# Clearing attention's query and key slabs on ScalarE during the first expert stage, with batch 0 normalised first and a store wait moved

## The chip, the cores and the metric

The kernel runs on 1 core of a Trainium2 chip. The metric is the device time of one execution in microseconds (us), taken as the median of several runs. The engines are PE (TensorE), DVE (VectorE), ACT (ScalarE), POOL (GpSimd) and SP (SyncE, which here only issues DMAs and waits).

## The reference, cut to what matters

Four residual blocks follow one another on x of shape (8, 512, 128), each behind a layer norm. Only the two in the middle, and the seam between them, are near the change.

```python
x = x + L0_attn(layernorm(x))     # a linear recurrence and a small MLP
x = x + L0_ffn(layernorm(x))      # 8 experts, top 2, gelu, hidden 256
x = x + L1_attn(layernorm(x))     # causal attention, 16 heads of 8
x = x + L1_ffn(layernorm(x))      # 8 experts, top 2, gelu, hidden 512, and a shared one

def L1_attn(x):                   # x: (8, 512, 128)
    q, k, v = heads(x @ Wq.T), heads(x @ Wk.T), heads(x @ Wv.T)
    logits = where(causal, q @ k.T * 8 ** -0.5, -max)
    return merge(softmax(logits) @ v) @ Wo.T
```

## The kernel before, in words

The kernel is a row of blocks (`nc.Block()`): `setup`, `lru_block`, `experts` for layer 0, `attention`, `route`, `experts` for layer 1. In a block each engine has a program of its own; the engines are tied by semaphores alone, and each works through its queue in order. At the end of a block every engine drains, they meet in a barrier, and only then does any of them start the next block.

**The expert stage (layer 0).** Before it tokens are sorted by expert into slots in DRAM (`xslots`), in two groups of four batches. `experts` walks over 10 bodies of 8 tiles. SP loads tiles to `xt`, PE transposes them, multiplies with the first weights into `hb` (gelu on ACT) and with the second into PSUM; DVE copies the result to `yb[r]`, and SP stores `yb[r]` to `yslots` (`store`, L996). At the head of the block DVE still sorts the second group (L319 to L381), POOL scatters its rows, and ACT has two short tasks: an exponential that waits for `exp_in` (L1067) and the first two weight copies (L1051). The first Gelu (L1082) waits for PE. POOL gathers the four batches of group 0 (L902) while the second group is computed, and DVE adds three of them to X at the end. The last thing in SP's program is a wait for both `stored` semaphores (L1028 and L1029): the last rows must have landed in `yslots`, since the next block gathers from there.

**Attention.** The queries and keys go through DRAM: `keep` stores the projected terms, `spread` reads them back, 32 small DMAs a batch, into slabs `Q` [128, 4, 512] and `KZ` [128, 16, 512], of which it fills only some rows. The other rows must be zero (in `KZ` also a constant from `sgn`), and they are written once, at the head of the block, by DVE (L1465, L1467, and four times L1472, one for each 32 partitions). Then DVE copies `identr` and clears `Mc`, and only then come `scales` (the reciprocal of the deviations, which waits for a square root on ACT, L273) and `normalise` for batch 0 (L747 to L752). PE transposes the normalised batch (`turn_in`, L1676), ACT copies it out (`to_xs`, L1600), PE projects keys and queries (L1681), ACT and DVE split each into a high and a low part (`upper`, L1607, and `lower`, L1484), SP stores and spreads them, and PE's first scores (L1695) wait for the first spread. POOL meanwhile clears `Vz` (L1440, L1444), normalises batch 1, lays the values out, and gathers batches 4 to 7 of the expert stage (L902), which DVE adds to X one after another within batch 0.

**Memory.** In the kernel before `Q` and `KZ` are buffers of `attention` alone, `yb` belongs to each expert stage, and `stage` (raw weights, 16 KB a partition) lives from `setup` to the end of the first expert stage.

Of the kernel before, what the change touches and what calls it, by code (L numbers as in the profile page):

```python
# [19 lines left out]
P = 128  # L20
# [3 lines left out]
E = 8  # L24
# [372 lines left out]
def lru_block(nc, s, A, sem, sb):  # L397
# [23 lines left out]
    flat = lambda t: t[:, :, :].rearrange("p j d -> p (j d)")  # L421
    tiles = lambda b: slice(TB * b, TB * b + TB)
    TURNS = B + 2

    RANK = GROUPS[0] + 2

# [508 lines left out]
        batch_stats(dve, s, b, 2)  # L935


def experts(nc, s, sem, layer, out=None):


# [2 lines left out]
    def sems(name, count):  # L943
        return [sem(f"{name}{k}{tag}") for k in range(count)]
# [5 lines left out]
    two = range(2)  # L950
    RING = 4
    scattered, stored = s.scattered, sems("stored", 2)
    sums = s.sums = Sums(sem, layer)

    x_load, loaded = s.x_load, 16 * BODIES * layer
# [29 lines left out]
    with nc.Block() as block:  # L985
        @block.sync
        def _(sp):
            def load(g, n, r):

                wait_apart(sp, x_turned, 2 * (n + BODY0[g]) + (r + 1))  # L990
                sp.dma_start(xt[r][:, :, :], xrows[g][:, bass.ds(BT * n + TB * r, TB), :]).then_inc(x_load[r], 16)

            def store(g, n, r):

                wait_apart(sp, yb_ready, 2 * (n + BODY0[g]) + (r + 3))
                sp.dma_start(yrows[g][:, bass.ds(BT * n + TB * r, TB), :], yb[r][:, :, :]).then_inc(stored[r], 16)  # L996

            def rows_in(g):
                sp.wait_ge(scattered[g], 16 * 2 * TB * GROUPS[g] * (layer + 1))

            rows_in(0)
            for r in two:
                load(0, 0, r)
            for g in range(NG):

                for r in two:
                    load(g, 1, r)
                    if g > 0:
                        store(g - 1, GB[g - 1] - 1, r)
                with sp.Fori(1, GB[g] - 1) as n:  # L1010
                    for r in two:
                        load(g, n + 1, r)
                        store(g, n - 1, r)
                if g + 1 < NG:
                    rows_in(g + 1)
                for r in two:
                    if g + 1 < NG:
                        load(g + 1, 0, r)
                    store(g, GB[g] - 2, r)
            for r in two:  # L1020
                store(NG - 1, GB[NG - 1] - 1, r)
            if layer == 1:

                for b in range(B):
                    sp.wait_ge(x_done, b + 1)
                    sp.dma_start(out[b].rearrange("(j p) d -> p j d", p=P), s.X[:, TB * b:TB * b + TB, :]).then_inc(x_out, 16)
                sp.wait_ge(x_out, 16 * B)
            for r in two:  # L1028
                sp.wait_ge(stored[r], 16 * BODIES)  # L1029

        @block.gpsimd
        def _(pool):
# [12 lines left out]
        def _(act):  # L1045
# [17 lines left out]
                    shared(b)  # L1063

            if layer == 0:
                act.wait_ge(exp_in, 1)
                act.activation(s.top[:, 1, :], s.top[:, 1, :], ACT.Exp).then_inc(exp_ready, 1)  # L1067
                warm(act, s, 0, ACT.Gelu)
                for t, e in enumerate(numbers(act, 0, 2)):
                    copy_down(0, t, e)  # L1070
# [244 lines left out]
def attention(nc, s, sem, sb):  # L1315
# [1 line left out]
    NCH = 5 * HG // 2  # L1317
    names = ("nb_ready", "turned", "xs_ready", "p_ps", "high_ready", "p_ready", "v_ps", "v_ready", "vz_ready", "s_ready",
             "s_read", "m_ready", "mh_ready", "mc_ready", "mt_ps", "q2_ready", "w_ready", "e_ready", "cut", "pv_ready", "o_ready", "ot_ps",
             "rd_ready", "a_ready", "at_ps", "af_ready", "wo_ps", "x_done", "slabs", "vz_zero", "ln_in")  # L1320
    q = {n: sem(n + "_t") for n in names}
    qk_in = [sem(f"qk_in{g}") for g in range(G)]
    kept = [sem(f"kept{k}") for k in range(2)]
    terms = [nc.dram_tensor(f"terms{k}", (B, 3 * P, T), F32, kind="Internal").ap() for k in range(2)]
    Q, KZ = sb("Q", [P, G, T], F32R), sb("KZ", [P, H, T], F32R)
    high, low = [[sb(f"{n}{k}", [P, T], F32R) for k in range(2)] for n in ("high", "low")]
    Vs = sb("Vs", [P, TB, P])
    Vz = sb("Vz", [P, TB, H, SLAB])
# [20 lines left out]
    with nc.Block() as block:  # L1349
        @block.sync  # L1350
        def _(sp):
            def keep(b):

                for k, parts in ((KEY, (high, high, low)), (QUERY, (high, low, high))):
                    wait_apart(sp, q["p_ready"], 2 * b + (k + 1))
                    for t, part in enumerate(parts):
                        sp.dma_start(terms[k][bass.ds(b, 1), P * t:P * t + P, :].rearrange("b p t -> (b p) t"),
                                     part[k][:, :].bitcast(F32)).then_inc(kept[k], 16)

            def spread(b, gg, used):  # L1360

                if gg == 0:
                    for k in (KEY, QUERY):
                        wait_apart(sp, kept[k], WRITES * b + WRITES)
                if used is not None:
                    wait_apart(sp, q["w_ready"], used)
                for g in range(HG):
                    rows = slice(SLAB * g, SLAB * g + 3 * DH)
                    for k, dst in ((QUERY, Q[rows, gg, :]), (KEY, KZ[rows, HG * gg + g, :])):
                        heads = terms[k][bass.ds(b, 1), :, :].rearrange("b (r h) t -> h (b r) t", h=H)  # L1370
                        sp.dma_start(dst.bitcast(F32), heads[G * g + gg, :, :]).then_inc(qk_in[gg], 16)

            sp.wait_ge(q["slabs"], 7)
            keep(0)
            for gg in range(G):
                spread(0, gg, None)
            with sp.Fori(0, B - 1) as b:
                keep(b + 1)
                for gg in range(G):
                    spread(b + 1, gg, NCH * G * b + NCH * (gg + 1))  # L1380
            for gg in range(G):
                sp.wait_ge(qk_in[gg], READS * B)

        @block.gpsimd
        def _(pool):
# [61 lines left out]
            norm_in(1, 1)  # L1447
            norm_rows(0, TB)
            spread(0, None)
            for b in range(FIRST[1], B):  # L1450
                gather(pool, s, s.sums, b)
                if b == B // 2 + 1:
                    norm_in(2, 2)
                    norm_rows(0, TB)
# [7 lines left out]
        @block.vector  # L1462
        def _(dve):
            dve.sem_inc(q["s_read"], 2)
            dve.tensor_copy(Q[:, :, :].rearrange("p G (t c) -> p (G t) c", c=P),  # L1465
                            s.zero[:, :].unsqueeze(1).broadcast_to([P, G * TB, P])).then_inc(q["slabs"], 1)
            dve.tensor_copy(KZ[:, :, :].rearrange("p h (t c) -> p (h t) c", c=P),  # L1467
                            s.zero[:, :].unsqueeze(1).broadcast_to([P, H * TB, P])).then_inc(q["slabs"], 1)
            dve.wait_ge(q["slabs"], 2)
            for g in range(HG):  # L1470
                rows = slab(g)
                dve.tensor_scalar(KZ[rows, g:H:HG, :].rearrange("p h (t c) -> p h t c", c=P),  # L1472
                                  s.zero[rows, :].unsqueeze(1).unsqueeze(1).broadcast_to([SLAB, G, TB, P]), s.sgn[rows, 2:3], None, ALU.add)\
                   .then_inc(q["slabs"], 1)
            dve.tensor_copy(identr[:, :], s.ident[:, :])
            dve.tensor_copy(Mc[:, :, :], s.zero[:, :].unsqueeze(1).broadcast_to([P, TB, P])).then_inc(q["slabs"], 1)
            scales(dve, s, 2)
            normalise(dve, s, nb, s.mu[1], s.r[1], 0, q["ln_in"], 1).then_inc(q["nb_ready"], 1)
            dve.wait_ge(q["slabs"], 7)

            def lower(b, k, ps):

# [380 lines left out]
def build(nc, A, out):  # L1863
    with ExitStack() as ctx:
# [33 lines left out]
        s.x_load = [sem(f"x_load{r}") for r in range(2)]  # L1898

        s.stats_sems = [sem(f"stats_{n}") for n in ("st", "mv", "std", "done")]  # L1900
        s.warmed = sem("warmed")
        s.route_sems = [sem(f"route_{n}") for n in ("exp_in", "exp_ready", "mb_ready", "rank_ps")]
        s.mb_ready, s.rank_ps = s.route_sems[2:4]
        s.rank_read, s.placed, s.route_chain = (sem(n) for n in ("rank_read", "placed", "route_chain"))
# [7 lines left out]
        s.mu, s.r = [sb(f"muc{k}", [P, TB]) for k in range(2)], [sb(f"rc{k}", [P, TB]) for k in range(2)]  # L1912
        s.rd = sb("rd", [P, TB * HG, 2])
        s.nb, s.xs = [sb(f"nb{k}", [P, TB, P]) for k in range(2)], [sb(f"xs{k}", [P, T]) for k in range(2)]
        s.b2row = s.bcast[:, 0:P].unsqueeze(1).broadcast_to([P, TB, P])

        def ffn(layer, start):

            with ExitStack() as own:
# [17 lines left out]
                s.xT = [fs(f"xT{layer}{k}", [P, T]) for k in range(2)]  # L1937
                s.wst = [fs(f"wst{layer}{k}", [P, NC * P]) for k in range(2 * TB)]
                s.hb = [fs(f"hb{layer}{k}", [P, NC * P]) for k in range(4)]
                s.yb = [fs(f"yb{layer}{k}", [P, TB, P]) for k in range(2)]  # L1940
                s.rk = fs(f"rk{layer}", [P, 2 * E * TB * max(GROUPS)])
                start()
                experts(nc, s, sem, layer, out)


# [3 lines left out]
        with ExitStack() as early:  # L1949
            es = allocator(early)  # L1950
            s.w1T, s.w2T = es("w1T", [P, E, F0 * P]), es("w2T", [P, E * F0, P])
            s.stage = es("stage", [P, 2 * E * F0, P])

            def first_stages():
                own_buffers(lambda nc, s, sem, sb: setup(nc, s, A, sem, sb))
                own_buffers(lambda nc, s, sem, sb: lru_block(nc, s, A, sem, sb))

            ffn(0, first_stages)
        own_buffers(attention)
        ffn(1, lambda: route(nc, s, sem))  # L1960


# [19 lines left out]
```

## Time and profile before

| | |
|---|---|
| median of 3 runs | 988.51 us (987.65 to 989.19) |
| the profiled execution | 990.38 us, of which the span from its first to its last instruction is 988.6 us |
| granted TensorE clock, mean over the span | 0.915 of full |
| the experts' last DVE instruction ends, attention's first instructions start | 252.2 us, 256.8 us |
| PE has nothing to do at this seam | 251.5 to 271.9 us |

Times of single instructions are read from the profiled execution, on a clock that starts with its span. An idle time in brackets is that of the engine before the instruction, with what ended it. A granted clock of 0.50 is TensorE at 1.2 GHz, 1.00 is 2.4 GHz.

### The profile page before, as it was taken

Reading aid. Unit: us, or ns where it says so; the run is one execution under the profiler, and the core shown is the slowest. Engines: PE = TensorE matmul, PEld = TensorE weight load, DVE = VectorE, ACT = ScalarE, POOL = GpSimd, SP = SyncE. Lnnn points to the kernel's source line nnn. Section 1 sums busy time; section 2 is a strip of 40 time slices with the busy share of each in tenths; the row PEclk is TensorE's granted clock in tenths of the full one; section 3 lists DMA queues with packets and bytes.
Section 4 is the critical chain, followed back from the end, with each engine's and each line's share of the span. In section 5 each row is a group of like instructions: output and inputs, shape, how many; then the busy total and the mean of one; then the engine's idle time right before and its main releaser. Section 6 shows DMA issues by size and latency. Waiting matters only on the chain. (4 is left out here: it accounts for less than half of the span.)

```text
span 988.6 us, 18788 instructions
## 1 busy us (share of the span) xinstructions
PE 808.0 (82%) x5585; PEld 601.9 (61%) x5585; DVE 637.7 (65%) x1445; ACT 503.9 (51%) x1081; POOL 417.4 (42%) x520
## 2 busy tenths in 40 slices
PE   2798816898159899999999999977278899999993
PEld 2566606898125456565555656546236899999862
DVE  4578643558729987777777777727721566568457
ACT  3475423565114566767767676664122366665520
POOL 3664567547277113232332332221167720273174
PEclk9999857999669999999999999995579899999997
DMA  5920014544144121313122131000012222242222
GB/s 156 366 81 1 30 47 137 160 141 138 30 149 134 44 84 43 99 32 99 44 96 76 51 99 46 17 1 0 6 48 72 94 80 75 81 116 76 78 61 69
DMA packets 82155, 80.45 MB, mean 81 GB/s; under 512 B 9856, under 2 KB 61758, under 8 KB 82110
## 3 DMA queue, kind: packets, MB, share of 16 engines
q1 hardware_dynamic: 73122, 62.68, 20.8%
q0 software_dynamic: 8192, 16.79, 5.8%
q10 hardware_dynamic: 796, 0.42, 0.2%
q8 instruction: 22, 0.36, 0.2%
q14 instruction: 23, 0.19, 0.1%
HBM read 41.06 MB, written 38.80 MB: 81 GB/s over the span
## 5 line engine op out<-in xcount | busy, mean ns | idle before, releaser
L1619 ACT ACTIVATE Pb<-ps,low 128x512 f32<-128x512 f32 x320 | 216.3, 688 | 134.0 <-PE ps L1718 87.6
L902 POOL DMA_INDIRECT YG<-yslots,slot x128 | 131.3, 1026 | 149.3 <-DMA yslots<-yb 78.9
L1497 DVE TENSOR_REDUCE m<-ps 128x4 f32<-128x1024 f32 x128 | 156.3, 1222 | 54.1 <-PE ps L1695 35.9
L1718 PE MATMUL ps<-Q,KZ 128*128 128x128 f32 (+3 forms) x512 | 172.2, 398 | 4.8 <-ACT Pb L1619 4.0
L390 POOL DMA_INDIRECT xslots<-XN,slot x128 | 124.0, 969 | 72.2 <-issue 37.5
L1421 POOL TENSOR_SCALAR_AFFINE_SELECT Pb<-Pb 128x512 f32<-128x512 f32 (+1 forms) x84 | 67.6, 804 | 190.8 <-ACT Pb L1619 190.2
L1263 PE MATMUL ps<-xT,wst 128*128 128x128 f32 x960 | 137.4, 282 | 7.8 <-DVE wst L1132 5.0
L1718 PEld LDWEIGHTS ps<-Q,KZ 128*128 128x128 f32 x512 | 93.1, 192 | 81.8 <-ACT Pb L1619 56.1
L1275 PE MATMUL ps<-wst,hb 128*128 128x128 f32 x960 | 134.0, 277 | 6.6 <-ACT hb L1082 6.1
L1085 ACT ACTIVATE hb<-ps,upb 128x128 f32<-128x128 f32 x320 | 91.3, 368 | 76.6 <-PE ps L1263 76.6
L1263 PEld LDWEIGHTS ps<-xT,wst 128*128 128x128 f32 x960 | 123.6, 198 | 9.5 <-DVE wst L1132 6.1
L1695 PE MATMUL ps<-KZ,Q 128*128 128x512 f32 x320 | 115.7, 440 | 14.5 <-DMA KZ<-terms 9.7
L1275 PEld LDWEIGHTS ps<-wst,hb 128*128 128x128 f32 x960 | 120.2, 193 | 8.3 <-DVE yb L1127 8.0
L1734 PE MATMUL ps<-Pb,Vz 128*32 128x512 f32 (+3 forms) x1024 | 88.8, 442 | 0.8 <-POOL Pb L1421 0.8
L1695 PEld LDWEIGHTS ps<-KZ,Q 128*128 128x128 f32 x320 | 59.0, 198 | 20.9 <-DMA KZ<-terms 9.9
L1082 ACT ACTIVATE hb<-ps 128x256 f32<-128x256 f32 x80 | 31.0, 387 | 46.5 <-PE ps L1263 42.7
L1132 DVE COPY wst<-up 128x512 f32 x80 | 35.0, 440 | 29.1 <-PE ps L1263 20.7
L1698 PE MATMUL ps<-later,identb 128*128 128x512 bf16 x128 | 50.9, 398 | 0.0
L1222 PE MATMUL ps<-xf,swup 128*128 128x512 f32 x64 | 36.2, 666 | 16.9 <-ACTq L1061 16.9
L1137 DVE COPY wst<-down 128x512 f32 x80 | 34.5, 437 | 22.3 <-PE ps L1275 22.2
L1058 ACT ACTIVATE hs<-ps,vec 128x512 f32<-128x512 f32 x32 | 22.0, 687 | 50.4 <-PE ps L1222 50.4
L1495 DVE TENSOR_REDUCE m<-ps 128x8 f32<-128x1024 f32 x32 | 39.2, 1224 | 10.0 <-PE ps L1698 7.3
(256 smaller groups left out, 1239.9 us busy)
## 6 DMA issues: line engine op xcount, KB each, us to landing
xt<-xslots SPq DMA_DIRECT2D x40, 256.0 KB
yslots<-yb SPq DMA_DIRECT2D x40, 256.0 KB, 2.3
terms<-high SPq DMA_DIRECT2D x32, 256.0 KB, 2.2
Q<-terms SPq DMA_DIRECT2D x128, 48.0 KB
KZ<-terms SPq DMA_DIRECT2D x128, 48.0 KB
xslots<-YG SPq DMA_DIRECT2D x2, 2560.0 KB, 11.8
terms<-low SPq DMA_DIRECT2D x16, 256.0 KB, 2.3
X<-in_L_attn_x_dram SPq DMA_DIRECT2D x4, 512.0 KB, 6.0
```

The lines of the kernel that those rows point to most:

```text
L390: pool.indirect_dma_start(out=s.xslots[g][:, :], out_offset=bass.IndirectOffsetOnAxis(ap=s.slot[:, k, j:j + 1], axis=0), in_=s.XN[:, j, :] ...
L902: pool.indirect_dma_start(out=s.YG[:, TB * w + j, k, :], out_offset=None, in_=s.yslots[group][:, :], in_offset=bass.IndirectOffsetOnAxis(a ...
L1085: m = act.activation(hb[t % RING][:, c * P:c * P + P], psH[t % RING][:, c * P:c * P + P], ACT.Gelu, bias=s.upb[:, bass.ds(of_tile[t] * NC ...
L1263: m = pe.matmul(psH[t % RING][:, c * P:c * P + P], up[t % RING][:, c * P:c * P + P], xT[r][:, (t % TB) * P:(t % TB) * P + P], start=True, ...
L1275: m = pe.matmul(psY[r][:, (t % TB) * P:(t % TB) * P + P], hb[t % RING][:, c * P:c * P + P], down[t % RING][:, c * P:c * P + P], start=(c = ...
L1421: pool.affine_select(out=v, in_=v, compare_op=ALU.is_ge, fill=0.0, base=0, pattern=[[0, 2 if part == 2 else 4], [0, 2 if part else 1], [1, ...
L1497: w = dve.tensor_reduce(top[:, :, (TB + 1, 3, TB, None, 1)[u]], ps.rearrange("p (t g k) -> p g t k", t=2, g=HG), AX.XY, ALU.max)
L1619: act.activation(Pb[:, NCH * (gg % 2) + c, :], bank(4 + c % 2), ACT.Exp, bias=s.low[:, :], scale=DH ** -0.5)\
L1695: last = pe.matmul(ps, Q[:, gg, qt * P:qt * P + P], KZ[:, HG * gg:HG * gg + HG, kt * P:kt * P + P], start=True, stop=qt != kt)
L1698: last = pe.matmul(ps, s.identb[:, :], s.later[:, :].unsqueeze(1).broadcast_to([P, HG, P]), start=False, stop=True)
L1718: w = pe.matmul(ps[:, col:col + T - kt * P], KZ[:, HG * gg + g, kt * P:kt * P + P], Q2[gg % 2][:, kt * P:T], start=True, stop=not masked)
L1734: w = pe.matmul(PV[slab(g), kt * P:T], Vz[:, kt, HG * gg + g, :], Pb[:, NCH * (gg % 2) + c, col:col + T - kt * P], start=(kt == 0 and gg % ...
```

## The change

1. `empty_slabs` clears `Q` and `KZ` on ACT, at the head of the block of `experts` for layer 0, ahead of ACT's wait for `exp_in`. It has six instructions (2048 and 8192 elements on 128 partitions, then four of 2048 on 32 partitions) and counts on a new semaphore `s.slabs`.
2. DVE's six instructions for the same work leave `attention`. There `scales` and `normalise` of batch 0 come first now, and `identr` and `Mc` behind them.
3. SP waits for the slabs behind `keep(0)` rather than ahead of it.
4. In layer 0 SP no longer waits for the last stores at the end of the block. POOL waits for them in `attention`, ahead of its gathers; `yb` is one pair of buffers for the whole kernel now, so the stores may run on into the next block.
5. `Q` and `KZ` are allocated from the other end of SBUF from the first expert stage on, and `stage` becomes a buffer of `lru_block` alone.

```diff
@@ lru_block
+    s.stage = sb("stage", [P, 2 * E * F0, P])
@@
+SLABS = 2 + HG
+
+def empty_slabs(act, s):
+    zero = s.zero[:, :]
+    act.activation(s.Q[:, :, :].rearrange("p G (t c) -> p (G t) c", c=P),
+                   zero.unsqueeze(1).broadcast_to([P, G * TB, P]), ACT.Identity).then_inc(s.slabs, 1)
+    act.activation(s.KZ[:, :, :].rearrange("p h (t c) -> p (h t) c", c=P),
+                   zero.unsqueeze(1).broadcast_to([P, H * TB, P]), ACT.Identity).then_inc(s.slabs, 1)
+    act.wait_ge(s.slabs, 2)
+    for g in range(HG):
+        rows = slice(SLAB * g, SLAB * g + SLAB)
+        act.activation(s.KZ[rows, g:H:HG, :].rearrange("p h (t c) -> p h t c", c=P),
+                       zero[rows, :].unsqueeze(1).unsqueeze(1).broadcast_to([SLAB, G, TB, P]), ACT.Identity,
+                       bias=s.sgn[rows, 2:3]).then_inc(s.slabs, 1)
@@ experts, sync
-            for r in two:
-                sp.wait_ge(stored[r], 16 * BODIES)
+            if layer == 1:
+                for r in two:
+                    sp.wait_ge(stored[r], 16 * BODIES)
@@ experts, scalar
             if layer == 0:
+                empty_slabs(act, s)
                 act.wait_ge(exp_in, 1)
@@ attention, sync
-            sp.wait_ge(q["slabs"], 7)
             keep(0)
+            sp.wait_ge(s.slabs, SLABS)
@@ attention, gpsimd
             spread(0, None)
+            for r in range(2):
+                pool.wait_ge(s.stored[r], 16 * BODIES)
             for b in range(FIRST[1], B):
                 gather(pool, s, s.sums, b)
@@ attention, vector
             dve.sem_inc(q["s_read"], 2)
-            dve.tensor_copy(Q[:, :, :]..., s.zero[:, :]...).then_inc(q["slabs"], 1)
-            dve.tensor_copy(KZ[:, :, :]..., s.zero[:, :]...).then_inc(q["slabs"], 1)
-            dve.wait_ge(q["slabs"], 2)
-            for g in range(HG):
-                rows = slab(g)
-                dve.tensor_scalar(KZ[rows, g:H:HG, :]..., s.zero[rows, :]..., s.sgn[rows, 2:3], None, ALU.add)\
-                   .then_inc(q["slabs"], 1)
-            dve.tensor_copy(identr[:, :], s.ident[:, :])
-            dve.tensor_copy(Mc[:, :, :], ...).then_inc(q["slabs"], 1)
             scales(dve, s, 2)
             normalise(dve, s, nb, s.mu[1], s.r[1], 0, q["ln_in"], 1).then_inc(q["nb_ready"], 1)
-            dve.wait_ge(q["slabs"], 7)
+            dve.tensor_copy(identr[:, :], s.ident[:, :])
+            dve.tensor_copy(Mc[:, :, :], ...).then_inc(s.slabs, 1)
+            dve.wait_ge(s.slabs, SLABS + 1)
@@ build
+        s.yb = [sb(f"yb{k}", [P, TB, P]) for k in range(2)]
...
-                s.yb = [fs(f"yb{layer}{k}", [P, TB, P]) for k in range(2)]
...
+                if layer == 0:
+                    s.Q = slabs.enter_context(nc.sbuf_tensor("Q", [P, G, T], F32R, side="right"))
+                    s.KZ = slabs.enter_context(nc.sbuf_tensor("KZ", [P, H, T], F32R, side="right"))
```

## Rows read from the trace of the kernel before

**Rows 1.** The page, busy time by engine.
```profile
PE 808.0 (82%) x5585; PEld 601.9 (61%) x5585; DVE 637.7 (65%) x1445; ACT 503.9 (51%) x1081; POOL 417.4 (42%) x520
```

**Rows 2.** Timeline, seam to attention: start us, us, engine, line, operation, idle before.
```profile
251.54 0.69 DVE L1127 COPY yb<-ps 128x512 f32<-128x512 f32 x1 [2.00 <-PE ps L1275]
256.81 1.28 ACT L273 ACT_TABLE_LOAD   x1 [6.22 <-PEq L985]
256.81 1.81 POOL L1440 MEMSET Vz<- 128x2048 f32 x1 [6.76 <-POOLq L985]
256.87 2.83 DVE L1465 CAST Q<-zero 128x2048 fp32r<-128x2048 f32 x1 [4.64 <-PEq L985]
258.10 0.30 ACT L273 ACTIVATE std<-mv,eps 128x12 f32<-128x12 f32 x1
258.68 1.17 POOL L1444 MEMSET Vz<- 128x32 f32 x2
259.62 4.50 DVE L1467 CAST KZ<-zero 128x8192 fp32r<-128x8192 f32 x1
264.16 5.21 DVE L1472 TENSOR_SCALAR KZ<-zero,sgn 32x2048 fp32r<-32x2048 f32 x4
...
269.88 0.22 DVE L284 RECIPROCAL rstd<-std 128x12 f32<-128x12 f32 x1
...
271.91 1.12 PE L1676 MATMUL ps<-ident,nb 128*128 128x128 f32 x4 [20.41 <-DVE nb L752]
```

**Rows 3.** Waits of SP's DMA queue, 240 to 300: total us, times, longest.
```profile
SPq L1029 <- DMA yslots<-yb: 1.9, 1, 1.9
SPq L985 <- PEq L985: 1.9, 1, 1.9
```

**Rows 4.** Line of the experts' block, up to 256.9: durations ns, first and last start.
```profile
L985 POOLq EVENT_SEMAPHORE  x2: 17/17/17, 256.5 to 256.6; - x2
L985 POOLq DRAIN  x1: 21654/21654/21654, 234.8 to 234.8; - x1
...
L985 SPq DRAIN  x1: 7/7/7, 254.8 to 254.8; - x1
```

**Rows 5.** The same line in the second expert stage, from 720 on.
```profile
L985 SPq DRAIN  x1: 7/7/7, 988.4 to 988.4; - x1
L985 SPq EVENT_SEMAPHORE  x1: 17/17/17, 988.5 to 988.5; - x1
```

**Rows 6.** Timeline, head of `route`.
```profile
671.04 1.28 ACT L273 ACT_TABLE_LOAD   x1 [4.53 <-PEq L1349]
...
672.69 0.35 DVE L284 RECIPROCAL rstd<-std 128x32 f32<-128x32 f32 x1 [2.01 <-ACT std L273]
...
674.85 1.12 PE L857 MATMUL ps<-ident,nb 128*128 128x128 f32 x4 [6.22 <-DVE nb L752]
```

**Rows 7.** Timeline of ACT, head of the first expert stage.
```profile
133.40 1.28 ACT L1067 ACT_TABLE_LOAD   x1 [6.42 <-PEq L434]
137.77 0.23 ACT L1067 ACTIVATE top<-top 128x32 f32<-128x32 f32 x1 [3.08 <-DVE top L1177]
...
140.02 0.20 ACT L296 ACTIVATE junk<-eps 128x1 f32<-128x1 f32 x1
158.84 0.38 ACT L1082 ACTIVATE hb<-ps 128x256 f32<-128x256 f32 x1 [18.62 <-PE ps L1263]
```

**Rows 8.** Groups of ACT by form: count, busy us, mean ns, idle before.
```profile
L1051 ACT COPY wst<-w2T 128x256 f32 x80 | 32.3, 405 | 7.4 <-PE ps L1275 0.7
...
L833 ACT ACTIVATE XN<-nb 128x512 f32 x8 | 5.0, 630 | 7.3 <-DVE nb L752 7.1
```

**Rows 9.** PE by stretch: us, busy (count), granted clock, DMA share, GB/s.
```profile
277.00:278.00 1.00, 1.00 (x7) 0.79 0.00 0
...
297.00:298.00 1.00, 1.00 (x2) 0.55 0.67 189
```

**Rows 10.** Timeline of PE, batch 0's first scores.
```profile
289.54 2.07 PE L1695 MATMUL ps<-KZ,Q 128*128 128x512 f32 x4 [9.70 <-DMA KZ<-terms]
```

More of the change, by code:

```diff
@@ L952, in experts @@
     scattered, stored = s.scattered, sems("stored", 2)
+    s.stored = stored
     sums = s.sums = Sums(sem, layer)
@@ L1319, in attention @@
              "s_read", "m_ready", "mh_ready", "mc_ready", "mt_ps", "q2_ready", "w_ready", "e_ready", "cut", "pv_ready", "o_ready", "ot_ps",
-             "rd_ready", "a_ready", "at_ps", "af_ready", "wo_ps", "x_done", "slabs", "vz_zero", "ln_in")
+             "rd_ready", "a_ready", "at_ps", "af_ready", "wo_ps", "x_done", "vz_zero", "ln_in")
     q = {n: sem(n + "_t") for n in names}
@@ L1324, in attention @@
     terms = [nc.dram_tensor(f"terms{k}", (B, 3 * P, T), F32, kind="Internal").ap() for k in range(2)]
-    Q, KZ = sb("Q", [P, G, T], F32R), sb("KZ", [P, H, T], F32R)
+    Q, KZ = s.Q, s.KZ
     high, low = [[sb(f"{n}{k}", [P, T], F32R) for k in range(2)] for n in ("high", "low")]
@@ L1464, in _ @@
             dve.sem_inc(q["s_read"], 2)
[L1465 to L1468, printed above, removed]
-            dve.wait_ge(q["slabs"], 2)
-            for g in range(HG):
-                rows = slab(g)
-                dve.tensor_scalar(KZ[rows, g:H:HG, :].rearrange("p h (t c) -> p h t c", c=P),
-                                  s.zero[rows, :].unsqueeze(1).unsqueeze(1).broadcast_to([SLAB, G, TB, P]), s.sgn[rows, 2:3], None, ALU.add)\
-                   .then_inc(q["slabs"], 1)
-            dve.tensor_copy(identr[:, :], s.ident[:, :])
-            dve.tensor_copy(Mc[:, :, :], s.zero[:, :].unsqueeze(1).broadcast_to([P, TB, P])).then_inc(q["slabs"], 1)
             scales(dve, s, 2)
             normalise(dve, s, nb, s.mu[1], s.r[1], 0, q["ln_in"], 1).then_inc(q["nb_ready"], 1)
-            dve.wait_ge(q["slabs"], 7)
+            dve.tensor_copy(identr[:, :], s.ident[:, :])
+            dve.tensor_copy(Mc[:, :, :], s.zero[:, :].unsqueeze(1).broadcast_to([P, TB, P])).then_inc(s.slabs, 1)
+            dve.wait_ge(s.slabs, SLABS + 1)
             def lower(b, k, ps):
@@ L1900, in build @@
         s.stats_sems = [sem(f"stats_{n}") for n in ("st", "mv", "std", "done")]
-        s.warmed = sem("warmed")
+        s.warmed, s.slabs = sem("warmed"), sem("slabs")
         s.route_sems = [sem(f"route_{n}") for n in ("exp_in", "exp_ready", "mb_ready", "rank_ps")]
@@ L1951, in build @@
             s.w1T, s.w2T = es("w1T", [P, E, F0 * P]), es("w2T", [P, E * F0, P])
-            s.stage = es("stage", [P, 2 * E * F0, P])
             def first_stages():
@@ L1956, in first_stages @@
                 own_buffers(lambda nc, s, sem, sb: lru_block(nc, s, A, sem, sb))
+            slabs = ctx.enter_context(ExitStack())
             ffn(0, first_stages)
         own_buffers(attention)
+        slabs.close()
         ffn(1, lambda: route(nc, s, sem))
```

## The prediction, made before the changed kernel was run

> **What bounds the kernel now.** I read the page first: PE is busy for 82% of the span [rows 1], so a gain has to come from a place where PE stands still and nothing else runs that must run. The timeline of the seam between the first expert stage and attention shows such a place: PE waits 20.41 us for the first normalised batch [rows 2]. In these 20.4 us there are two pieces. From 251.5 to 256.8 no engine has started attention. From 256.87 to 269.88 DVE writes constants into Q and KZ, and identr and Mc, while PE, ACT and (from 259.9 on) POOL have nothing to do; the square root that the reciprocal needs is ready at 258.40. Then come 2.03 us from the reciprocal to PE's first transpose. So this seam is a plain chain: barrier, DVE's constants, normalise, PE. What comes behind hangs on it with relative waits only: PE's first scores wait for the spread of the terms of batch 0 [rows 10], which start from the same transpose, and POOL's normalising of batch 1 and its gathers wait for the same transpose too.
>
> I then asked which engine the barrier waits for. The waits of SP's queue show 1.9 us for the last store at L1029, and after it another 1.9 us in the barrier [rows 3]. The line of the block says why: SP drains at 254.8, but POOL's drain, which is 21.65 us long from 234.8, ends at 256.45, and the release follows at 256.5 to 256.7 [rows 4]. Where SP comes last, at the end of the kernel, the release is 0.1 us behind it [rows 5]. So SP's store wait is covered here by POOL's drain, with 1.6 us to spare.
>
> **The change part by part.** *Six DVE instructions leave attention's head, and normalise moves ahead of identr and Mc.* Before, from ACT's table load to PE's transpose it is 271.91 - 256.81 = 15.10 us [rows 2]. The head of route runs just the sequence that is left (table load, square root, reciprocal, two small copies, the copy of X, four subtractions and products, PE's transpose) with nothing ahead of it: 674.85 - 671.04 = 3.81 us [rows 6]. Its reciprocal is over 32 columns and takes 0.35 us, attention's over 12 takes 0.22 [rows 2, 6], so 3.68 us. I take 3.7. Gain: 15.1 - 3.7 = 11.4 us. identr and Mc, 0.5 us, now run on DVE while PE transposes and projects; DVE's next task, the low part of the keys, came 4.6 us after normalise, so they are hidden, and without that cover they would cost 0.5.
>
> *POOL beside DVE at the head.* Before, Q took 2.83 us for 2048 elements, while KZ took 4.50 for 8192, which is 1.13 for 2048: Q stood for about 1.7 us beside POOL's 1.81 us memset. POOL's two memsets of 32 elements, 1.17 us together, likewise end only when Q has ended [rows 2]. In the new order DVE's first instruction comes 1.65 us after the block's start, when the large memset has 0.2 us to go; the two small ones follow. I charge nothing for it; the bounds are 0 and the 1.2 us that the two small ones took.
> The Trainium skill says the same of these two engines (SBUF — State Buffer, "SBUF: two separate sides"): they share one port pair under an exclusive lock, and the loser blocks for the whole instruction; by that rule the trace agrees, and ACT has a port of its own, so that the slabs on ACT disturb nobody.
>
> *The table load is newly bare.* In the old order ACT's table load and square root, 1.6 us, lay under DVE's constants; now they open the chain, and they are inside the 3.7 us. The row gives 1.28 us for the load and the square root directly behind it [rows 2, 6].
> The Trainium skill (ScalarE: Activation LUTs, "What ACT_TABLE_LOAD costs") gives about 2.66 us for a switch of tables, drain included; with it the gain would be 10.0 rather than 11.4. The two heads in this trace show no such drain in front of DVE's start, so the row decides.
>
> *Six ACT instructions at the head of the first expert stage.* Together they have 2048 + 8192 + 4 x 2048 = 18432 elements a partition. A 256-element copy takes 0.405 us and a 512-element one 0.630 [rows 8]: 0.88 ns an element and 0.18 fixed, so 6 x 0.18 + 18432 x 0.88 ns = 17.3 us. They start at 133.4 with the block and end near 150.7. Behind them in ACT's queue stand the exponential, the table loads, the copies for the first two tiles, and a second warm-up: from 137.77 to 140.22 that is 2.45 us, plus the first table load of 1.28, which before ran in the wait [rows 7], so 154.4; some 1.1 us of register loads (what DVE needed for a like step) make it 155.5. ACT is next needed at 158.84 [rows 7]. Cover left: 3.3 us, so the cost is nothing. The exponential, 14 us late now, is next read by DVE at 159.93. Bounds: nothing; and, if each 512 elements cost the full 0.630 us, 22.7 us, an end at 160.9 and 2.1 us lost.
>
> *SP's store wait leaves the block's end, and POOL waits ahead of its gathers.* At most it gives back 1.9 us [rows 3]. As POOL's drain is what ends last [rows 4], I take 0. POOL's new wait is passed long after the last store has landed (before 254.8, when SP was through), since the gathers start some 20 us into attention; nothing queues behind it. Bounds: 0 and 1.9 us gained.
>
> *SP's slab wait behind keep(0), and the new places in SBUF*: the slabs are long ready, so both cost 0.
>
> *TensorE's clock.* PE's granted clock is 0.50 at the restart at 271.91 and rises at about 277.4; after the next rest it is 0.50 from 289.54 and rises at about 297.9 [rows 9]. So a rise came 5.5 to 8.4 us after PE's restart, for no reason that lies in the kernel's order. When all of attention starts 11.4 us earlier, each later rise can fall up to 3 us earlier or later relative to the work, and PE at half clock loses half of that: 1.5 us either way at the first scores, about 1 at the start of the second expert stage. I take 0, and 2 us either way for both.
>
> **Sum.** 11.4 + 0 + 0 + 0 = 11.4 us. Against the profiled execution 990.38 - 11.4 = 979.0, span 977.2. This execution lies 1.87 above the median of the runs shown, so the median should be 988.51 - 11.4 = 977.1 us. The own range of this case is 977.1 - 2.2 to 977.1 + 2.2.
>
> **Rivals.**
> 1. *The barrier moves as well.* POOL's drain ends 6.4 us after its last gather instruction, and I can't say from the trace what holds it. If that is tied to the stores or to SP, the whole block ends 1.9 us earlier. Against it: the last store had landed before 254.8, and the drain ended 1.6 us later. Time: 988.51 - 13.3 = 975.2.
> 2. *Part of the gain is lost at once*: DVE stands behind POOL's memsets in the new order (1.2), or ACT is late for the first Gelu (2.1), or the clock falls badly (2). Two of them together leave a gain of about 7: 981.5.
> 3. *Slower: ACT's slabs don't fit.* Place: the head of the first expert stage. If ACT needs more than 1.83 ns for an element, the six instructions last longer than 17.3 + 3.3 + 11.4 + 2 = 34 us, and the Gelu at 158.84 comes so late that the time is over 990.5. At 2.0 ns they take 37.9 us, and the time is 977.1 + 17.3 = 994.4. For it: no row shows ACT on a tile over 512 elements or with such a broadcast source. Against it: all its rows are near 0.9 ns.
> 4. *Nothing comes of it*: the 11.4 us come back as a wait in batch 0 of attention, for the gathers of batches 4 to 7 on POOL. Against it: POOL starts them from the same transpose, so they come 11.4 us earlier too, and the trace has no wait of DVE for a gather there. Time: 988.5.
>
> **How the numbers follow.** Forecast 0.63, rival 1 0.18, rival 2 0.10, rival 3 0.05, rival 4 0.04. Likeliest 977.1. The range goes from 973.0 (rival 1 with a good clock) to 981.5 (rival 2), and leaves out rivals 3 and 4 and the tails. About 0.2% (2 us) is what a measurement can tell from no change. Faster: 0.63 + 0.18 + 0.10 = 0.91; same 0.04; slower 0.05.
>
> **What would show it.** In the new profile: (a) the barrier releases at 256.7 as before, SP's queue having come 3.5 us ahead of it; (b) ACT's table load to PE's first transpose is 3.7 us; (c) six ACT instructions of about 2.0 (five) and 7.4 us (one) from 133.4 on, done by 151, and the first Gelu at 158.8 still waits for PE; (d) PE's idle time at the seam is 9.0 us instead of 20.4; (e) PE's first scores come at 278.1 rather than 289.5, still behind the spread; (f) the distance from that point to the end of the span is unchanged within 2 us. The prediction is wrong if the release moves, if the Gelu waits on ACT, or if a clock rise moves more work than I allowed.

## The result

The changed kernel takes 979.8 us (median of 6 runs, 973.6 to 983.1) against 989.88 for the kernel before in the same session: ratio 0.9891, interval 0.9856 to 0.9927. Measured once more it gave 981.67 against 990.98, ratio 0.9915 (0.9897 to 0.9934). By the ratios it is faster by 10.8 and 8.4 us, by the medians by 10.1 and 9.3, where 11.4 were forecast. The first interval, 7.2 to 14.3 us, holds 11.4; the second, 6.5 to 10.2, doesn't. The time forecast was 977.1 us, with a range of 973.0 to 981.5; 979.8 lies inside it and 981.67 just above. Of the first miss of 2.7 us, 1.4 come from the kernel before, whose median was 989.88 here and 988.51 in the runs that the forecast started from. The profiled execution, 973.6 us, is the fastest of its six, and 5.4 us below the 979.0 that the sum gave for it; the stage table below shows where those 5.4 us lie.

The timeline of the seam after the change, against [rows 2]:

```profile
248.13 0.69 DVE L1149 COPY yb<-ps 128x512 f32<-128x512 f32 x1 [1.99 <-PE ps L1297]
253.39 1.28 ACT L273 ACT_TABLE_LOAD   x1 [6.22 <-PEq L1005]
253.41 1.81 POOL L1462 MEMSET Vz<- 128x2048 f32 x1 [6.75 <-POOLq L1005]
254.69 0.30 ACT L273 ACTIVATE std<-mv,eps 128x12 f32<-128x12 f32 x1
255.03 0.23 DVE L284 RECIPROCAL rstd<-std 128x12 f32<-128x12 f32 x1 [6.21 <-ACT std L273]
255.27 0.21 POOL L1466 MEMSET Vz<- 128x32 f32 x2
...
257.06 1.12 PE L1690 MATMUL ps<-ident,nb 128*128 128x128 f32 x4 [8.97 <-DVE nb L753]
...
261.69 0.69 DVE L1498 SCALAR_TENSOR_TENSOR low<-high,ps 128x512 fp32r<-128x512 f32 x1 [4.21 <-ACT high L1621]
```

From the table load to PE's first transpose it is 257.06 - 253.39 = 3.67 us, and PE's idle time has gone from 20.41 to 8.97. The two small memsets take 0.21 us, not 1.17: no large copy of DVE stands in their way. DVE's own end to the table load is 253.39 - 248.82 = 4.57 us, as before (256.81 - 252.23 = 4.58). The line of the experts' block, and SP's waits, against [rows 3, 4]:

```profile
L1005 POOLq EVENT_SEMAPHORE  x2: 17/17/17, 253.1 to 253.2; - x2
L1005 POOLq DRAIN  x1: 21652/21652/21652, 231.4 to 231.4; - x1
...
L1005 SPq DRAIN  x1: 124/124/124, 249.3 to 249.3; - x1
```
```profile
SPq L1005 <- PEq L1005: 3.9, 1, 3.9
```

SP now drains at 249.3 and waits 3.9 us in the barrier, where it had waited 1.9 for the store and 1.9 in the barrier. POOL's drain still ends last (231.4 + 21.65 = 253.05). ACT at the head of the first expert stage, against [rows 7]:

```profile
131.67 1.91 ACT L945 ACTIVATE Q<-zero 128x2048 fp32r<-128x2048 f32 x1 [6.86 <-PEq L435]
133.49 7.01 ACT L947 ACTIVATE KZ<-zero 128x8192 fp32r<-128x8192 f32 x1
140.53 8.07 ACT L952 ACTIVATE KZ<-zero,sgn 32x2048 fp32r<-32x2048 f32 x4
148.62 1.28 ACT L1089 ACT_TABLE_LOAD   x1
...
157.25 0.38 ACT L1104 ACTIVATE hb<-ps 128x256 f32<-128x256 f32 x1 [4.88 <-PE ps L1285]
```

The six instructions last from 131.67 to 148.6, 16.9 us, and ACT still idles 4.9 us before the first Gelu.

To see where the time of one execution goes I took the release of each block's barrier (the semaphore rows of the block's line) in every profile, and in attention the first score and the first matmul of the softmax weights on PE. All in us:

| profile | recurrence stage | experts 0 | attention | of it: to first score | to first weights | rest | route | experts 1 |
|---|---|---|---|---|---|---|---|---|
| before | 112.3 | 123.4 | 414.2 | 32.8 | 13.6 | 367.8 | 51.7 | 265.9 |
| before, again | 112.1 | 123.4 | 414.4 | 32.9 | 13.6 | 367.9 | 51.7 | 265.7 |
| changed | 110.4 | 121.8 | 401.4 | 21.2 | 12.5 | 367.7 | 51.9 | 265.0 |
| changed, again | 111.9 | 122.8 | 405.2 | 21.4 | 15.6 | 368.2 | 51.9 | 264.1 |

The distance to the first score falls by 11.4 to 11.7 us. In the first profile of the changed kernel 1.9 us more come from the recurrence stage, whose instructions the change doesn't touch and which took 111.9 the second time. The other stages give the rest: 1.6 in the first expert stage, 0.9 in the second, and the remainder in attention behind the first score. What differs most between the two profiles of one kernel is the next stretch, 12.5 against 15.6 us. The second profile is an execution of 979.2 us, the fastest of its five, and 11.2 below the 990.38 of the kernel before: in attention it gains 9.0 us, not 11.4, and 1.6 to 1.8 more come from the second expert stage.

### The profile page after: what moved, and what is told of

It reads as the page before. It is cut to its first block and busy times, and to the rows that moved or that the text cites. A ratio compares the mean times of both kernels' runs of the same rounds, so it can differ in the third digit from the quotient of the medians.

```text
span 971.7 us, 18786 instructions
## 1 busy us (share of the span) xinstructions
PE 802.5 (83%) x5585; PEld 598.1 (62%) x5585; DVE 625.6 (64%) x1439; ACT 521.4 (54%) x1087; POOL 418.5 (43%) x520
## 3 DMA queue, kind: packets, MB, share of 16 engines
q0 software_dynamic: 8192, 16.79, 5.7%
## 5 line engine op out<-in xcount | busy, mean ns | idle before, releaser
L1709 PE MATMUL ps<-KZ,Q 128*128 128x512 f32 x320 | 113.5, 433 | 14.1 <-DMA KZ<-terms 8.7
L1709 PEld LDWEIGHTS ps<-KZ,Q 128*128 128x128 f32 x320 | 58.0, 195 | 20.3 <-DMA KZ<-terms 9.0
## 6 DMA issues: line engine op xcount, KB each, us to landing
xslots<-YG SPq DMA_DIRECT2D x2, 2560.0 KB, 11.7
```

The costliest lines, as they stand in the source:

```text
L1709: last = pe.matmul(ps, Q[:, gg, qt * P:qt * P + P], KZ[:, HG * gg:HG * gg + HG, kt * P:kt * P + P], start=True, stop=qt != kt)
```

## The experiments

All ratios are to the kernel before, run beside them.

**1. The changed kernel again.** No edit.

> The changed kernel once more. The prediction's theory: the change is worth the 11.4 us at attention's head and nothing else, so the time is 11.4 us (plus or minus 2) below the kernel before, although the profiled execution of the changed kernel was 16.8 us shorter; the other 5.4 us lie in stages that the change doesn't touch and vary from run to run. Rival: the change also shortens other stages (the new places in SBUF, the earlier start), then the difference is near 16.8 us here too, and the stages before attention take 20 + 110.4 + 121.8 us again.

Ratio 0.9915 (0.9897 to 0.9934), 981.67 us. The rival falls: the 16.8 us belonged to one execution. The difference is 8.4 us by the ratio and 9.3 by the medians, so it misses the 11.4 and its 2 us of tolerance by a little. The second profile shows what attention loses: after the first score PE's clock behaves otherwise. The same four matmuls of the first unit take 2.07 and 2.08 us, but then:

```profile
277.07 1.10 PE L1709 MATMUL ps<-KZ,Q 128*128 128x512 f32 x2
```
```profile
280.14 2.10 PE L1709 MATMUL ps<-KZ,Q 128*128 128x512 f32 x3
...
290.34 0.79 PE L1709 MATMUL ps<-KZ,Q 128*128 128x512 f32 x1 [0.47 <-DVE m L1511]
```

The first row is the first profile of the changed kernel, with two scores matmuls in 1.10 us; the other two are the second profile, with three in 2.10 and, 13 us after the first score, one of 0.79 where it takes 0.49 to 0.50 at full clock. PE by stretch in this second profile (columns as in [rows 9]):

```profile
283.00:284.00 1.00, 1.00 (x5) 0.70 0.67 189
286.00:287.00 1.00, 0.25 (x3) 1.00 0.51 162
293.00:294.00 1.00, 1.00 (x3) 0.58 0.00 0
```

The clock rises at 283.6, falls again at 287.0 (the step is in the next stretch), and rises at 293.8: 6.0, 9.4 and 16.2 us behind the first score. In the first profile it rose 3.4 us behind it and stayed up for 51 us.

**2. SP's store wait back at the block's end**, all else as changed.

```diff
-            if layer == 1:
-                for r in two:
-                    sp.wait_ge(stored[r], 16 * BODIES)
+            for r in two:
+                sp.wait_ge(stored[r], 16 * BODIES)
```

> The changed kernel with SP's wait for the last stores back at the end of the first expert stage's block. Theory: POOL's drain ends last there, so the barrier is released at the same distance behind DVE's last instruction (4.5 us) as with the change, SP comes 1.6 us before the release, and the time equals that of the changed kernel within 0.3 us. Rival: the wait holds the barrier; then the release is 1.9 us later and the time 1.9 us longer.

Ratio 0.9894 (0.9874 to 0.9915), 979.29 us: the changed kernel's, within both intervals. In its profile SP drains at 255.0 and POOL's drain ends at 235.0 + 21.65 = 256.65; the release is at 256.7. Against the changed kernel in the same session (0.9915) the rival would have given 0.9934, which lies outside this interval.

**3. The store wait alone moved, on the kernel before** (SP's wait out, POOL's in ahead of its gathers, `yb` shared).

> The kernel before with one part of the change: SP no longer waits for the last stores, POOL does ahead of its gathers, and yb is shared. Theory: POOL's drain ends last, so the release stays 4.5 us behind DVE's last instruction and the time is that of the kernel before, within 0.3 us. Rival: 1.9 us faster.

Ratio 0.9999 (0.9986 to 1.0011) over 12 runs. The interval leaves at most 1.4 us, so the rival's 1.9 are excluded: that part of the change is worth nothing, as forecast.

**4. Batch 3 gathered in attention**, on the changed kernel, which takes POOL's last eight gathers out of the block, once without and once with SP's store wait.

```diff
-                for b in range(FIRST[g], FIRST[g] + GROUPS[g]):
+                for b in range(FIRST[g], FIRST[g] + GROUPS[g] - (layer == 0)):
                     gather(pool, s, sums, b)
@@ attention, gpsimd
-            for b in range(FIRST[1], B):
+            for b in range(FIRST[1] - 1, B):
                 gather(pool, s, s.sums, b)
```

> The changed kernel with the eight gathers of batch 3 moved from the first expert stage to attention, ahead of those of batch 4. Theory: POOL's drain follows its last gather by some 6.4 us, so it ends 10 us earlier, at about 3.5 us before DVE's last instruction, and the barrier then waits for DVE and SP alone: release about 0.2 us behind SP's last issue, 0.7 us behind DVE's last instruction instead of 4.5. Gain 3.7 us on the changed kernel, 15 on the kernel before, if POOL's eight more gathers (10 us) in attention stay ahead of DVE's sums, which they led by 27 us. Rival 1: the drain ends at a fixed distance from the end of the block or of DVE's work, not from the gathers: no gain. Rival 2: the sums of batch 0 in attention wait for the gathers: the 3.7 us go there.

> As the kernel with the late gathers, but with SP's store wait back at the end of the block. Theory: now nothing covers the wait, so SP comes last, and the barrier is released 1.9 us later than without the wait, 2.6 us behind DVE's last instruction; time 1.9 us over that of the kernel with the late gathers. Rival: if the store wait is worth nothing even then, both are equal.

The block's line without the store wait, and SP's waits with it:

```profile
L1005 POOLq EVENT_SEMAPHORE  x2: 17/17/17, 251.5 to 251.5; - x2
L1005 POOLq DRAIN  x1: 21609/21609/21609, 222.7 to 222.7; - x1
...
L1005 DVEq DRAIN  x1: 723/723/723, 250.2 to 250.2; - x1
...
L1005 SPq DRAIN  x1: 123/123/123, 251.3 to 251.3; - x1
```
```profile
SPq L1049 <- DMA yslots<-yb: 1.9, 1, 1.9
SPq L1005 <- PEq L1005: 0.2, 1, 0.2
```

POOL's drain now ends at 244.35, 5.8 us behind its last gather (238.57) instead of 6.4, and SP is last: without the wait the release comes 0.2 us behind it, and 0.6 us behind DVE's last instruction, where 0.7 was expected. With the wait SP is last too, and spends 1.9 us on the store; the release is 2.6 us behind DVE's last instruction, as expected. The expert stage takes 118.7 us without the wait, 121.0 with it, 122.8 in the changed kernel. So what POOL's drain covers, and what the wait costs once it is bare, came out as expected: the wait is worth 2 us only after the drain has been moved away.

The whole time did not follow. The ratios are 0.9874 (0.9845 to 0.9903) without the wait and 0.9846 (0.983 to 0.9862) with it: the kernel that should be 1.9 us slower has the lower median, 976.37 against 979.23, though the intervals overlap and don't settle the order. Against the changed kernel in the same session (0.9897 to 0.9934) the one with the wait is faster; the one without is 4.1 us better by the ratio, but its interval overlaps. In the profiles attention takes 407.5 us without the wait and 405.4 with it, and 1.8 of the difference is again the stretch behind the first score, 15.4 against 13.6.

**5. Normalise first, DVE still clears**, on the kernel before: `scales` and `normalise` stand ahead of the two large copies, and nothing else differs.

> The kernel before with one part of the change: batch 0 is normalised first, and DVE still clears the slabs behind it. Theory: PE's first transpose comes 3.7 us after the block's start as in the changed kernel, but DVE's next step of the chain, the low part of the keys, waits until the constants are written: 3.7 + 1.1 + 4.5 + 5.2 + 0.5 = 15.0 us after the start instead of 19.7. So the first scores come 4.7 us earlier than before, and the time is 4.7 us below the kernel before: the rest of the 11.4 us needs the move to ACT. Rival: POOL's normalising of batch 1 (3.9 us) now runs beside DVE's large copies; if the two block each other, as Q's copy and the memset did, the gain shrinks to about 1 us.

Ratio 0.9971 (0.9959 to 0.9982), so 2.9 us, not 4.7. The timeline:

```profile
258.62 1.22 DVE L1467 CAST Q<-zero 128x2048 fp32r<-128x2048 f32 x1
...
259.75 4.42 DVE L1469 CAST KZ<-zero 128x8192 fp32r<-128x8192 f32 x1
...
260.07 4.15 POOL L1390 COPY muc<-mv 128x4 f32<-128x4 f32 x1 [2.90 <-PE ps L1676]
...
264.21 5.53 DVE L1474 TENSOR_SCALAR KZ<-zero,sgn 32x2048 fp32r<-32x2048 f32 x4
...
270.50 1.29 DVE L1484 SCALAR_TENSOR_TENSOR low<-high,ps 128x512 fp32r<-128x512 f32 x2
```

The chain came out as worked: the low parts start 270.50 - 255.09 = 15.4 us after ACT's table load instead of 19.7, and the first score 28.6 us after the release instead of 32.8, 4.2 less. The rival fell: it was POOL that waited, 4.15 us for a copy of four elements, and nobody needed it. But the stretch behind the first score is 16.0 us instead of 13.6, and the rest 1.5 longer: in this profile the clock is low until 19 us behind the first score. Attention in that profile keeps 0.3 to 0.5 of the 4.2 us; the runs keep 2.9.

**6. KZ cleared once more on ACT.** One more copy of that instruction, and a wait for it.

> The changed kernel with KZ cleared twice on ACT, 7.0 us more at the head of the first expert stage. Theory: ACT stood idle 4.9 us before the first Gelu in the changed kernel, of which about 1.1 us are register loads, so the first Gelu comes 2.1 to 3.3 us late and ends an idle time of nothing on ACT, and the stage and the time grow by that. Rival: the stage has slack of its own behind the first Gelu, and the time stays.

ACT in this kernel, head of the first expert stage:

```profile
162.31 0.20 ACT L296 ACTIVATE junk<-eps 128x1 f32<-128x1 f32 x1
164.05 0.38 ACT L1107 ACTIVATE hb<-ps 128x256 f32<-128x256 f32 x1 [1.54 <-issue]
```

The idle time ahead of the first Gelu no longer waits for PE but is ACT's own 1.54 us of issue. Of the 4.88 us of cover 4.88 - 1.54 = 3.34 were free, so the Gelu is 7.03 - 3.34 = 3.7 us late, a little more than the 2.1 to 3.3 expected, since the issue takes 1.54 and not 1.1. The stage took 127.5 us, 4.7 more than the changed kernel's second profile; the 1.0 beyond the Gelu's delay came with a mean granted clock of 0.86 in the stage instead of 0.89. The ratio is 0.9926 (0.9911 to 0.994), 983.5 us: its interval and the changed kernel's overlap, so the loss is shown in the trace and only likely in the time.

**7. The kernel before, again.**

> The kernel before once more, for a second profile of it. If the clock's rises and falls alone make the stages vary, its attention stage, 414.2 us in the first profile, will differ by up to 3 us while the distance from the block's start to PE's first score stays 32.8 us; if not, both are equal within 0.5 us. Its time is that of the kernel before: ratio 1.000.

Ratio 1.0005. Its stages are those of the first profile within 0.2 us, and its clock steps too (a rise 12.2 us ahead of the first score, a fall 5.4 ahead, a rise 8.3 behind, against 12.1, 5.3 and 8.4), and so in the profile of experiment 3. My expectation of a variation was wrong for these profiles: the clock took the same course three times. In the kernel's other executions the clock did vary: the twelve here took 988.40 to 994.12 us, at mean granted clocks from 0.908 to 0.918.

**8. PE kept busy in the gap ahead of the first scores**, on the changed kernel.

```diff
+            def idle(n):
+                for _ in range(n):
+                    pe.matmul(bank(4), s.ident[:, :], s.lam[:, :], start=True, stop=True)
...
             turn_in(1)
+            idle(14)
             for u in range(NU):
                 row_scores(0, 0, u, 0)
```

> The changed kernel with 14 matmuls of constants (128x512, result never read) on PE between the transposes of batch 1 and the first scores, where PE stood idle for 9 us and the clock fell 7 to 8 us before the first score. Theory (the clock takes part of the gain and makes the runs vary): at full clock the 14 take 6 to 7 us and fit into the gap; the clock stays up through the first scores, PE's stretch from the first score to the first weights matmul is 12 us in every run instead of 12.5 to 16, the median is 1 to 3 us below the changed kernel and the runs lie within 4 us of each other rather than 9. Rival: DVE's maxima bound this stretch, or the spread of the runs comes from elsewhere; then the time is that of the changed kernel (or up to 3 us longer where the 14 don't fit).

```profile
267.74 12.18 PE L1850 MATMUL ps<-lam,ident 128*128 128x512 f32 x28
279.36 1.50 PE L1709 MATMUL ps<-KZ,Q 128*128 128x512 f32 x4
```

I had the size wrong: a matmul in 32-bit floats is two instructions, 0.87 us together at full clock, so the 14 took 12.2 us and pushed the first score 2.3 us back (23.7 against 21.4 us from the release). The clock stayed up, and the stretch behind was 12.2 us. Ratio 0.9892 (0.9873 to 0.9911), runs between 978.2 and 980.9, 2.7 us apart where the changed kernel's were 9.5 and 5.6. The interval overlaps both of the changed kernel's (0.9891 and 0.9915), so the gain of 1 to 3 us that I expected is not shown in the time: the 2.3 us of late start stand against what the clock gives.

**9. One more such matmul behind each of eight units of scores**, on the kernel of experiment 8.

> As the kernel with the busy gap, and one more such matmul behind each of eight of the first nine units of scores, where PE waits for DVE's maxima. Theory: the clock doesn't fall again 9 to 10 us behind the first score, as it did in two of the profiles, so this kernel is up to 1 us faster than the one with the busy gap alone. Rival: each extra matmul (0.43 us) holds back the next scores, and it is 1 to 3 us slower.

Ratio 0.9932 (0.9915 to 0.9949). The stretch took 14.2 us, 1.9 more than in experiment 8, with the clock up in both: the rival was right, the extra work held back the scores.

**10. Late gathers, no store wait, busy gap; with 14 and with 10 extra matmuls.**

> The kernel with batch 3's gathers in attention and no store wait of SP, with the busy gap. Theory: the 4 us that the earlier release gave (stage of 118.7 us against 122.8) stay now, as the clock no longer takes them: 13.5 us under the kernel before for the late gathers, 2 more for the clock, so some 975. Rival: with the clock held up the batch sums wait for the gathers, and nothing comes on top of the busy gap.

> The kernel with the late gathers and the busy gap, with 10 of the extra matmuls instead of 14. Each took 0.87 us (28 instructions in 12.18 us for 14), so the 14 ran 2.3 us over the gap of 9.7 us; 10 take 8.7 us and fit. Theory: the first score comes 21.5 us after the block's start again instead of 23.9, the clock stays up, and the time is 2.3 us below that of the kernel with 14: some 972.7, 17 below the kernel before. Rival: the 1 us that PE rests now lets the clock fall, or the gathers hold the sums, and the time stays near 975.

```profile
264.39 8.75 PE L1850 MATMUL ps<-lam,ident 128*128 128x512 f32 x20
272.57 1.48 PE L1709 MATMUL ps<-KZ,Q 128*128 128x512 f32 x4
```

974.99 us, ratio 0.9844 (0.9824 to 0.9864), and 972.43 us, ratio 0.9834 (0.9807 to 0.986). With 10 the matmuls fit (8.75 us), the first score is 20.3 us behind the release, the stretch 12.1. Five of its six runs lie between 970.95 and 973.41, at mean granted clocks of 0.929 to 0.935; one is at 979.69, at 0.924. Both lie below the changed kernel's second interval (0.9897 to 0.9934) and touch its first (0.9856 to 0.9927) at the edge. Between each other, and against both kernels of experiment 4, the intervals overlap, so what the busy gap adds to the late gathers is not shown in the time. These extra matmuls compute nothing that is used.

## Why the prediction held, and what it mis-sized

*Attention's head, 11.4 us.* Right. The head took 3.67 us where 3.7 was taken from route's head, and the first score came 11.4 to 11.7 us closer to the release. Normalise first alone gives 4.2 of it (experiment 5), the move of the slabs to ACT the rest.

*POOL beside DVE, the bare table load.* Right, both at 0: the load is 1.28 us, with the square root directly behind it (253.39 + 1.28 = 254.67, and it starts at 254.69), so the 2.66 us of the Trainium skill (ScalarE: Activation LUTs, "What ACT_TABLE_LOAD costs") did not appear in this head either.

*ACT's slabs cost nothing.* Right: 16.9 us against 17.3, and 3.3 us of free cover measured against 3.3 worked out. Experiment 6 used it up. Rival 3, which needed 34 us, is excluded.

*SP's store wait gives 0.* Right, and the cause was the one named: experiments 2 and 3 show no effect of the wait either way, and experiment 4 shows 2 us in the stage as soon as POOL's drain is out of its way. Rival 1 is excluded.

*The clock, taken as 0 plus or minus 2.* This is the term that was mis-sized: in its width, as the profiles show, and by the medians, which gain 8 to 11 us of the 11.4, in its centre too. In the second profile of the changed kernel attention is 9.0 us shorter: 11.4 less to the first score, 2.0 more behind it, 0.4 more in the rest. Where the clock was held up (experiments 8 and 10) the stretch behind the first score was 12.1 to 12.3 us in three profiles; where it was not it was 12.5 to 16.0 in ten (13.6 in all three of the kernel before and of the one with the store wait alone moved). That the low clock lengthens this stretch is shown by that.

The rest of attention also moved, between 367.7 and 370.8 us, and that too lies where the clock was low. PE by stretch in the two profiles of the changed kernel (columns as in [rows 9]): the first 100 us from the first score, and a stretch further back between two executions of the same four transposes (L1690 here), in which the clock was never low.

```profile
274.53:374.53 100.00, 90.91 (x584) 0.97 0.27 84
378.80:556.60 177.80, 175.08 (x1202) 1.00 0.22 71
```
```profile
277.60:377.60 100.00, 91.37 (x552) 0.90 0.28 84
386.50:564.20 177.70, 175.01 (x1202) 1.00 0.23 71
```

The same points in eight of the profiles, in us:

| profile | granted clock, 100 us from the first score | first score to the first of these transposes | from there to the second |
|---|---|---|---|
| experiment 8 | 0.98 | 104.2 | 177.6 |
| changed | 0.97 | 104.3 | 177.7 |
| before | 0.94 | 105.6 | 177.7 |
| experiment 2 | 0.92 | 106.7 | 177.7 |
| experiment 4, with the wait | 0.91 | 108.0 | 177.7 |
| changed, again | 0.90 | 108.9 | 177.7 |
| experiment 5 | 0.89 | 109.5 | 177.7 |
| experiment 4, without | 0.88 | 110.5 | 177.6 |

With the clock up, this stretch took 177.6 to 177.7 us in all fourteen profiles. In front of it the distance follows the clock, over 6.3 us. Not all of the difference need be the clock's: the two kernels of experiment 10, with late gathers, took 105.4 and 105.3 us at 0.97, where the changed kernel took 104.3.

So the 1.5 us either way that the prediction allowed at the first scores were too few: against the 105.6 of the kernel before, the two profiles of the changed kernel took 1.3 less and 3.3 more. Sign (f) of the prediction held all the same, with 697.2 and 699.8 us from the first score to the end of the span against 699.0, since the second profile gained again at the end of attention and in the second expert stage. The whole times point the same way. Of the changed kernel's eleven runs the five with a mean granted clock of 0.919 or more took 973.6 to 980.2 us, the six below it 980.4 to 984.8. Only two of the eleven have a profile, each the fastest of its group, so that the clock makes up the medians' shortfall of 1 to 3 us is likely and not shown.

*The other rivals, and luck.* Rival 4 is excluded by the time. Of rival 2, neither of the losses of DVE and ACT came, and the clock's did in one profile. Its 981.5 us is nearer to the second median than the forecast's 977.1, so the time alone would not have told the two apart; the profiles did. That the first profiled execution was 16.8 us faster and not 11.4 was luck: its recurrence stage was 1.9 us shorter, and its clock rose early at the first scores.

## What to carry to other kernels

Before a wait at a block's end is priced, read when each engine's drain ends: the wait named in the profile may be covered by a drain that no group of instructions shows, and it becomes worth something only when that drain has moved. Work without inputs, such as clearing buffers, belongs on an engine that idles in an earlier stage, and the room for it is the idle time less that engine's own issue time. A gain of a few microseconds ahead of PE's work may be partly taken back by the clock, so measure the stretch behind the edit too, compare a stretch with the clock at full in both profiles, and don't read a gain from one profile.

## What the runs showed of the hardware

- POOL's drain ended 6.4 us behind its last gather before the change and after it, and 5.8 us with 24 gathers instead of 32, while behind the recurrence stage's scatters it ended 2.1 us after the last one. What it does in that time stayed open.
- A POOL copy of 4 elements took 4.15 us beside DVE's 4.42 us copy, and 0.18 us alone.
- The clock can stay low over 19 us in which PE is busy for 8.48 of the first 10 and 8.54 of the next 9 (experiment 5). It could also fall again 3.4 us after a rise, in the middle of the first scores (experiment 1).
- ACT's table load took 1.28 us behind running instructions too: in the changed kernel the last clearing instruction ended at 148.60, the load began at 148.62, and the next instruction at 149.91.
